# Where the filter's bias is added: in SBUF, or in place in PSUM, in a graph network of eight passes over the edges

## The reference

```python
rbf = jnp.exp(coeff * (edge_attr[:, None] - offsets[None, :]) ** 2)
for i in range(DEPTH):                                  # DEPTH = 5
    W = ssp(rbf @ fw1[i] + fb1[i]) @ fw2[i] + fb2[i]    # the filter, one row of 128 per edge
    W = W * C[:, None]
    h = x @ lin1_w[i]
    msg = h[src] * W                                    # the message
    agg = jax.ops.segment_sum(msg, dst, num_segments=n) / denom
    x = x + ssp(agg) @ lin2_w[i] + lin2_b[i]
    x = layernorm(x) * ln_g[i] + ln_b[i]
```

## Time and profile before

| | us |
|---|---|
| median of three runs | 4603.52 |
| lowest, highest | 4602.52, 4611.04 |
| the profiled execution | 4598.03 |
| its span, first to last instruction | 4596.2 |

### The profile page before, as it was taken

One profiled execution on the slowest core, in us unless ns is written; L12 is line 12 of the kernel. 1 busy time (PEld: TensorE's weight loads), 2 busy tenths in 40 slices (PEclk: granted clock), 3 DMA queues, 4 the chain that ended last, 5 costly groups with the idle time before them and its releaser, 6 DMA issues. The chain is left out here.

```text
span 4596.2 us, 51942 instructions
## 1 busy us (share of the span) xinstructions
PE 2524.6 (55%) x13213; PEld 2251.8 (49%) x13213; DVE 2082.9 (45%) x4555; ACT 1837.8 (40%) x4373; POOL 3302.7 (72%) x3337
## 2 busy tenths in 40 slices
PE   3454456666566665666556665566663333333333
PEld 2444456655455554555555554566662333323333
DVE  4222255554555546555555555555553344421111
ACT  2112146665565645565456564555551111100000
POOL 5777767776777767777677776777753777767776
PEclk9999987776677766777667776766665555555555
DMA  6333222222222212222222222222211222212222
GB/s 136 90 98 96 71 58 68 70 69 51 64 68 67 69 47 68 68 69 67 55 62 67 68 67 55 60 65 67 64 42 30 55 57 56 57 43 56 55 56 53
DMA packets 194095, 297.28 MB, mean 65 GB/s; under 512 B 81758, under 2 KB 116680, under 8 KB 193788
## 3 DMA queue, kind: packets, MB, share of 16 engines
q0 software_dynamic: 106496, 219.17, 19.1%
q10 hardware_dynamic: 33942, 57.75, 4.4%
q1 hardware_dynamic: 53350, 16.87, 1.5%
HBM read 271.98 MB, written 21.57 MB: 64 GB/s over the span
## 5 line engine op out<-in xcount | busy, mean ns | idle before, releaser
L576 POOL DMA_INDIRECT rows<-table,staged_src x3328 | 3301.7, 992 | 1280.1 <-issue 888.9
L727 PE MATMUL pD<-scatter,msg 128*128 128x80 f32 x4160 | 774.9, 364 | 716.8 <-PEq L725 710.8
L727 PEld LDWEIGHTS pD<-scatter,msg 128*128 128x128 f32 x4160 | 733.2, 273 | 786.0 <-issue 786.0
L666 PE MATMUL pD<-scatter,rows 128*128 128x80 f32 x2496 | 573.0, 424 | 887.7 <-PEq L664 540.1
L666 PEld LDWEIGHTS pD<-scatter,rows 128*128 128x128 f32 x2496 | 544.1, 330 | 919.0 <-issue 919.0
L714 PE MATMUL pC<-fw,hidden 128*128 (+1 forms) x4160 | 809.9, 370 | 187.7 <-PEq L712 185.3
L714 PEld LDWEIGHTS pC<-fw,hidden 128*128 128x128 f32 x4160 | 755.3, 278 | 222.5 <-issue 221.5
L894 ACT ACTIVATE scatter<-onehot,c_e 128x80 f32<-128x80 bf16 x2080 | 549.5, 346 | 484.2 <-ACTq L892 483.6
L1226 DVE TENSOR_TENSOR msg<-msg,rows 128x512 f32<-128x512 f32 x520 | 336.4, 688 | 646.1 <-DVEq L1034 629.5
L1030 DVE COPY staged_src<-src_i 128x8 int32<-128x8 int32 x416 | 74.3, 179 | 727.5 <-DVEq L1038 727.5
L876 ACT ACTIVATE hidden<-hidden 128x512 f32<-128x512 f32 x520 | 327.5, 630 | 62.3 <-ACTq L779 1.6
(11 more groups left out here) (190 smaller groups left out, 1570.4 us busy)
## 6 DMA issues: line engine op xcount, KB each, us to landing
rows<-table,staged_src POOLq DMA_INDIRECT x3328
basis<-basis_d ACTq DMA_DIRECT2D x130, 256.0 KB, 2.8
table<-node_rows SPq DMA_DIRECT2D x66, 128.0 KB
msg<-in_edge_weight_dram ACTq DMA_DIRECT2D x54, 128.0 KB, 3.0
basis_d<-basis ACTq DMA_DIRECT2D x26, 256.0 KB, 3.6
hidden<-in_edge_weight_dram ACTq DMA_DIRECT2D x48, 128.0 KB, 3.3
out_dram<-node_rows SPq DMA_DIRECT2D x12, 128.0 KB
table<-node_rows SPq DMA_DIRECT2D x11, 132.0 KB
```

What stands on the lines that cost most here:

```text
L576: pool.indirect_dma_start(out=rows[:, s, j, 0:width], out_offset=None, in_=tab[:, :], in_offset=bass.IndirectOffsetOnAxis(ap=staged_src[:, ...
L666: mm = pe.matmul(sum_ps, rows[:, g % RING, j, 0:D], scatter[:, g % 2, j, :], start=(j == 0), stop=(j == CH - 1))
L727: mm = pe.matmul(sum_ps, msg_of(g, h)[:, c * D:(c + 1) * D], scatter[:, g % 2, HALF * h + c, :], start=(h == 0 and c == 0), stop=(h == 1 a ...
```

## The change

`take_filters` now adds the bias in place in the PSUM bank, and ends with `own`. `messages` reads that bank and the gathered rows, and writes `msg`. The bank is therefore read by the product last, and `filt_free` is gone: `filters` waits for `msg_full` instead, for one half of the group before for its first bank and for two for its second, without taking from the semaphore, since `message_sums` takes from it later. On DVE `take_filters(g+1)` moves behind `softplus_rest(g+2)` and `match(g+1)`.

```diff
@@ PE, filters(l, g) @@
                         pe.wait_ge(ssp_full, 1)
                         pe.sem_inc(ssp_full, -1)
-                        pe.wait_ge(filt_free, 1)
-                        pe.sem_inc(filt_free, -1)
+                        if g > 0:
+                            pe.wait_ge(msg_full, h + 1)
...
@@ DVE @@
-                dve.sem_inc(filt_free, 2)
...
                         dve.wait_ge(filt_full, 1)
                         dve.sem_inc(filt_full, -1)
+                        part = filt_ps[h].rearrange("p (c d) -> p c d", d=D)
+                        ins = dve.tensor_tensor(part, part, over_tiles(fb2[:, l, :], HALF), ALU.add)
+                    own(ins)
+
+                def messages(g):
+                    for h in range(2):
                         dve.tensor_tensor(msg_of(g, h).rearrange("p (c d) -> p c d", d=D),
                                           filt_ps[h].rearrange("p (c d) -> p c d", d=D),
-                                          over_tiles(fb2[:, l, :], HALF), ALU.add).then_inc(filt_free, 1)
-
-                def messages(g):
-                    for h in range(2):
-                        part = msg_of(g, h).rearrange("p (c d) -> p c d", d=D)
-                        dve.tensor_tensor(part, part, rows[:, g % RING, h * HALF:(h + 1) * HALF, 0:D], ALU.mult)\
-                           .then_inc(msg_full, 1)
+                                          rows[:, g % RING, h * HALF:(h + 1) * HALF, 0:D], ALU.mult).then_inc(msg_full, 1)
...
@@ DVE, conv_edges @@
-                            if g + 1 < GROUPS:
-                                take_filters(l, g + 1)
                             if g + 2 < GROUPS:
                                 softplus_rest(g + 2)
                             if g + 1 < GROUPS:
                                 match(onehot[:, (g + 1) % 2, :, :], g + 1).then_inc(onehot_full, 1)
+                                take_filters(l, g + 1)
```

More of the change, by code:

```diff
@@ L222, in build @@
         filt_full = sem("filt_full")
-        filt_free = sem("filt_free")
         msg_full = sem("msg_full")
```

## The result

| | us |
|---|---|
| after, median of four runs | 5196.32 (5190.23 to 5199.56) |
| before, median of the runs beside it | 4603.34 (4602.52 to 4611.04) |
| ratio, with its 95% interval | 1.1282 (1.1263 to 1.1302) |
| span of the profiled execution | 5194.1 instead of 4596.2 |

The changed kernel is 593 us slower; 504 were forecast (5107). The span grew by 598, and the passes of the five convolutions by 594 of these: 118, 109, 109, 103 and 155.

The account below looks back on a forecast made before the run. Gathers on POOL were taken to bound four convolutions, the computing engines the fifth. With the new wait chaining PE to DVE, 4598.0 + 376 (four convolutions) + 127 (fifth) = 5101, as median 5107 us; range 4980 to 5260 at 0.70.

Parts of the forecast that it names:

- The place of the bound: Convolutions: bound moves from POOL's gathers to the PE, ACT and DVE loop, 24.0 us a pair of groups instead of 20.3.
- The rival of the gather-bound pass: Convolutions: PE's work still fits beside DVE's waits, a pair stays at 20.3 us, 4565 us in all; chance 0.04.
- end of the filters to ACT: Even step: PE makes hidden units until ACT starts, 2.17 us at the low clock, 1.25 at the high.
- ACT to the sum add: Even step: ACT's first two strips until DVE ends the second 4.40 us, then 0.66, one-hot 0.81, bias adds 1.28, offset load 0.75.
- rows that overlap: Whole pair: a row starts 0.1 to 0.2 us before the one ahead ends, three or four times, 22.4 to 22.0.
- node work on DVE: Between an add and the next product: 4.3 us for each of 12 blocks over 26 pairs, 2.0 us a pair.
- the weighting by the mean clock: PE's terms: full clock in 44% of the time, from the mean granted clock 0.72, weighting pairs of 24.9 and 19.3 us.
- the surcharge: Fifth convolution: more node work in its loop adds 3.5 us to the 24.0 of a pair, giving 27.5.
- The wider bound of 1.62: DVE's two in-place bias adds of a group: 1.28 us taken, 1.62 the upper end, from the 128x640 tile at 0.81 each.
- The relief: POOL's gathers are no longer lengthened by the product, now with one PSUM input: 39 us of POOL's time at most, booked at nothing.
- The clock that rises: Rival: PE holds its full clock, 20.8 us a pair, 4700 us; chance 0.11 for times between it and the forecast.
- the one that stays low: Rival: PE's clock stays low, 26.4 us a pair, 5410 us; chance 0.14 for times between it and the forecast.

Follow-up runs that it names:

- e8_no_add: The changed kernel with the convolutions' bias adds and the wait for their completion left out, the offset load kept: 4854.3 us.
- e1_order: The kernel before with only DVE's bias add, still into SBUF, moved behind the rest of the softplus and the one-hot tile: 4583.2 us.

## Why the prediction held, and where it was short

**The place of the bound.** Right. Filters waited for the product, POOL idled 119 to 129 us behind four passes (117 forecast), rows were no longer waited for, and the ends of the passes did not move. In the fifth POOL did wait for slots of the ring, up to 11.0 us at a time. The rival of the gather-bound pass fell.

**The terms of a pair.** Means over convolution 3, by the prediction's own steps, in us (ACT's first operation is where a strip starts):

| | forecast | measured |
|---|---|---|
| even: product to filters | 0.84 | 0.74 |
| filters | 3.07 | 3.48 |
| end of the filters to ACT | 1.77 | 1.94 |
| ACT to the sum add | 7.90 | 8.11 |
| to the next product, no node work | 0.59 | 0.59 |
| odd: product to filters | 0.84 | 0.74 |
| filters | 3.07 | 3.72 |
| sums | 2.93 | 2.23 |
| to the add, to the product | 1.44 | 1.45 |
| rows that overlap | -0.4 | in the above |
| node work on DVE | 2.0 | 1.7 |
| pair | 24.0 | 24.6 |

**The step that failed is the weighting by the mean clock.** The mean was right, 0.71 instead of 0.72. But I gave every matmul the same share of the full clock. The filters stand right behind PE's idle stretch and run at 1.2 GHz: in 39 of convolution 3's 51 steps they take 3.7 to 3.8 us, in 4 only the 2.05 of the full clock. That is +1.06 a pair. The sums stand last in the busy stretch and run mostly at 2.4 (1.91 to 2.95 us in the odd steps), -0.70. With the hidden units +0.17 and smaller terms both ways, that is the 0.6 a pair: the hit on the pair is in part luck, since two errors of one cause cancelled. Seen by the runs, the shortfall lies with the late adds: the forecast without its 2.03 for them is 22.0 a pair, and e8_no_add took 21.8, while the adds took 2.8 with all that hangs on them. The 0.6 a pair gives 0.6 x 25.5 x 4 = 61 us of the 89 that were missing. One sum in the prediction is off: its pairs of 25.3 and 29 add up to about 5277, not 5260.

**The fifth convolution.** 28.6 instead of 27.5, the other 28 us. Over the 24.6 of the others it has 4.0, where I took 3.5 over 24.0: 1.9 for node work on DVE (3.6 instead of 1.7), 1.6 because ACT starts 3.5 us behind the filters instead of 1.9, 0.5 on PE's filters and sums. I had taken the surcharge as one figure from the pair before, without the ACT part. The timeline of ACT after shows what holds it in one even step of the fifth convolution:

```profile
3724.88 0.26 ACT L813 ACTIVATE node_rows<-pD,gate_b 128x2 f32<-128x2 f32 x1 [10.74 <-ACTq L812]
3726.26 0.38 ACT L819 ACTIVATE score<-pD 128x256 f32<-128x256 f32 x1 [1.12 <-ACTq L818]
3726.98 2.12 ACT L893 ACTIVATE scatter<-onehot,c_e 128x80 f32<-128x80 bf16 x8 [0.33 <-ACTq L891]
3729.00 0.66 ACT L874 ACTIVATE hidden<-pA,fb_l 128x512 f32<-128x512 f32 x1
```

ACT waits for the scores (`node_scores`), which PE makes behind the filters and hidden units, then weights the one-hot tile, and comes to the first strip late and without idling. In 9 of the 25 even steps it starts the strip so, 5.9 to 7.0 us behind the filters; in the third convolution in none. No run took the scores off this path.

**The bias add in place.** 1.28 for two was taken and 1.29 measured (0.692 each by the page; 0.680 before). The wider bound of 1.62 is refuted. The load behind it was taken at 0.75, and adds and load together at 2.03; without adds and `own` 2.26 went in one step and 2.3 in the mean. That both stand on the chain behind the new wait was in the prediction, but not how much hangs on it: 341 us with the wait, -20 without.

**The relief.** Booked at nothing, and that held, since the gathers were not the bound. Gathers that start inside a product were lengthened before and are not now. Timeline of POOL after, the first inside the product of 2091.77, the second inside the one-hot tile of 2094.36:

```profile
2092.03 0.95 POOL L575 DMA_INDIRECT rows<-table,staged_src  x1 [0.30 <-issue]
...
2094.53 1.46 POOL L575 DMA_INDIRECT rows<-table,staged_src  x1 [0.30 <-issue]
```

Counted over convolution 3: before, 51 gathers started inside a product, and 46 of them were lengthened, by 5.9 us together; after, 42 did and none was. The Trainium skill (SBUF — State Buffer, "Who interferes with whom") says that a VectorE instruction with two SBUF inputs contends with a GpSimd instruction that reads SBUF, and one with at most one SBUF input, outside the two-port modes, does not. The trace agrees. What the rule does not tell is who takes the place: the one-hot tile, with two SBUF inputs still, lengthened gathers by 5.5 us before and by 12.0 after. Before, 2 gathers started in its first 0.25 us, after it was 19. The sum is 24 us in this pass as before, and over all passes POOL's gathers are busy 3293.7 us instead of 3301.7: the relief came to next to nothing even in POOL's own time.

**The other rivals.** The clock that rises (4700) and the one that stays low (5410) both fell with the mean of 0.71. The wait binds in every step but the first of a pass.

## What to carry to other kernels

A shared buffer that is freed one step later costs what its next writer has queued behind it: here not the filters alone but the hidden units and sums behind them. The first repair to try is to move work that does not need the buffer ahead of the wait; it gave back 479 of 593 us. An add in place also brings a wait for its own completion, here 1.05 us with the load behind it, that is free only where it lies beside another engine's work. Edits are not additive when one of them moves the bound: an order that gained 20 us before the wait cost 341 behind it. And where an engine's clock follows its load, take each of its groups from a row with the same place behind the idle stretch, not by the mean clock of the loop.

## What the runs showed of the hardware

- A delay on another engine came back with interest through TensorE's clock: with 2.3 us more on DVE's path the granted clock of the even steps was 0.72 in the mean instead of 0.81, and PE's part of the path was 0.6 us longer.
- The mean granted clock of a whole execution can mislead. Three executions of the kernel before with 0.696 to 0.698 took 4594.4, 4604.0 and 4600.8 us, the others, with 0.63, 4596.0 to 4611.3. In the traces the difference lies ahead of the convolutions: over the first pass, from its first gather to the next pass's, the clock on record is 1.00 before and 0.52 in e1_order, yet the same 1421 matmuls were busy 267.1 and 266.7 us and the pass took 550.8 and 551.0.
- An add of 128x512 f32 in place in PSUM takes 0.692 us, from PSUM to SBUF 0.680. The Trainium skill (VectorE: DVE Perf Modes, the section on the TRN2 errata) has 691 ns for an f32 add of 512 elements; both rows lie within 2% of it, and for the length of the add itself the place hardly matters.
- A gather's instruction on POOL that started inside a DVE operation with two SBUF inputs took as long as if it had been held until that operation ended. In convolution 3 of both kernels, 96 gathers were lengthened so, 46 by products and 50 by one-hot tiles, and every one ended 0.81 to 0.82 us after the DVE operation, however early it had started. The earlier it started, the more it lost: up to 1.61 us instead of 0.94 in a one-hot tile, 1.30 in the shorter product.
